# First pass of a two-layer graph kernel: the row gather adds in place onto the edge features

## The reference

```
h   = relu(layernorm(x))
msg = h[src] + edge_attr                       # first pass: node row plus edge row
agg = segment_sum(msg, dst)
x   = x + batchnorm(relu(agg @ W1 + b1) @ W2 + b2)
h   = relu(layernorm(x))
x   = x + layernorm_graph(gcn2(relu(gcn1(h)))) # second and third pass: weighted sums of h[src], no edge features
```

## Time and profile before

| what | us |
|---|---|
| median of 3 runs (lowest to highest) | 2736.61 (2732.78 to 2737.00) |
| the profiled execution | 2731.35 |
| its span from first to last instruction | 2730.00 |
| PE busy | 2450.0 |
| POOL busy | 1920.0 |
| DVE busy | 1509.8 |
| ACT busy | 1323.0 |

### The profile page before, as it was taken

One profiled execution on the slowest core, in us unless ns is written; L12 is line 12 of the kernel. 1 busy time (PEld: TensorE's weight loads), 2 busy tenths in 40 slices (PEclk: granted clock), 3 DMA queues, 4 the chain that ended last, 5 costly groups with the idle time before them and its releaser, 6 DMA issues.

```text
span 2730.0 us, 67333 instructions
## 1 busy us (share of the span) xinstructions
PE 2450.0 (90%) x26318; PEld 2369.3 (87%) x26318; DVE 1509.8 (55%) x3805; ACT 1323.0 (48%) x3271; POOL 1920.0 (70%) x1833
## 2 busy tenths in 40 slices
PE   1399899999999999965999999999969999999996
PEld 0298899888898889855999999999969999999996
DVE  8898899888898889844333433333302222222212
ACT  8588788888888888855432433423200000000001
POOL 5777877777777777702777777777437777777772
PEclk9999999999999999967999999999979999999998
DMA  4566566666566666636566565665676666565654
GB/s 111 134 179 175 168 178 175 169 187 177 162 184 179 184 170 175 176 113 206 196 230 201 186 221 191 198 219 180 216 194 211 209 216 214 198 205 190 211 197 140
DMA packets 339567, 506.63 MB, mean 186 GB/s; under 512 B 277602, under 2 KB 283160, under 8 KB 313905
## 3 DMA queue, kind: packets, MB, share of 16 engines
q1 hardware_dynamic: 270454, 292.79, 34.4%
q0 software_dynamic: 57952, 89.89, 14.7%
q10 hardware_dynamic: 10840, 119.53, 11.6%
HBM read 364.94 MB, written 137.13 MB: 184 GB/s over the span
## 4 chain that ended last, share of the span: by engine, by line
PE 55%; POOL 19%; DVE 8%; issue 7%; ACT 6%; DMA 4%; SPq 1%; DVEq 0%; ACTq 0%; POOLq 0%
PE psum L1118 38%; POOL arena L1297 19%; PE psum L1098 5%; PE psum L1140 4%; PE psum L1133 3%; DMA arena<-in_edge_attr_dram 3%; ACT arena L1230 2%; DVE arena L964 2%; ACT arena L1217 1%; PE psum L1076 1%; DVE arena L990 1%; PE psum L1153 1%; DMA arena<-table,srcT 1%; PE psum L1156 1%; SPq L1312 1%
## 5 line engine op out<-in xcount | busy, mean ns | idle before, releaser
L1297 POOL DMA_INDIRECT arena<-table,srcT x1770 | 1839.9, 1040 | 650.2 <-issue 606.6
L1118 PE MATMUL psum<-arena 125*125 125x193 bf16 (+1 forms) x19600 | 1974.5, 247 | 44.4 <-DMA arena<-counts 22.9
L1118 PEld LDWEIGHTS psum<-arena 125*125 125x125 fp8e4 x19600 | 1860.1, 137 | 53.3 <-DMA arena<-counts 23.3
L1230 ACT ACTIVATE arena<-psum 125x500 uint16<-125x500 f32 (+1 forms) x923 | 662.9, 718 | 436.1 <-PE psum L1098 431.8
L1217 ACT ACTIVATE arena<-iota,modT 128x125 uint8<-128x125 f16 x1775 | 602.9, 391 | 2.1 <-ACT arena L1230 2.1
L964 DVE TENSOR_SCALAR arena<-iota,keyT,oddT 128x300 f16<-128x300 f16 x1775 | 575.7, 357 | 22.3 <-PE psum L1098 18.8
L1098 PE MATMUL psum<-arena 128*125 128x300 f16 x1775 | 524.2, 297 | 54.5 <-ACT arena L1230 34.1
L1279 ACT ACTIVATE cneg<-cst 125x1 f32<-125x1 f32 x25 | 5.1, 203 | 689.3 <-DVE arena L1051 689.3
L1098 PEld LDWEIGHTS psum<-arena 128*125 128x125 fp8e4 x1775 | 243.4, 137 | 100.2 <-DVE arena L964 70.8
L974 DVE SCALAR_TENSOR_TENSOR arena<-relT,psum 128x960 bf16<-128x960 f16 x272 | 308.9, 1136 | 0.0
L990 DVE TENSOR_TENSOR arena<-arena 128x650 f32<-128x650 f32 x334 | 273.0, 817 | 14.2 <-DMA arena<-in_edge_attr_dram 13.9
(11 more groups left out here) (222 smaller groups left out, 1014.1 us busy)
## 6 DMA issues: line engine op xcount, KB each, us to landing
arena<-counts SPq DMA_DIRECT2D x125, 1600.0 KB
counts<-arena ACTq DMA_DIRECT2D x71, 1600.0 KB
arena<-in_edge_attr_dram SPq DMA_DIRECT2D x166, 320.0 KB
arena<-table,srcT POOLq DMA_INDIRECT x1770
table<-arena SPq DMA_DIRECT2D x8, 1050.0 KB
table<-arena SPq DMA_DIRECT2D x25, 168.0 KB
arena<-table SPq DMA_DIRECT2D x4, 1050.0 KB
arena<-in_x_dram ACTq DMA_DIRECT2D x4, 700.0 KB
```

The lines of the kernel that those rows point to most:

```text
L1118: last = pe.matmul(ps_v[n % 2][0:PN, 0:xc], A(slot)[0:PN, j, 0:PN], Xs[0:PN, j, 0:xc], start=(j == 0), stop=(j == J - 1))
L1230: act.activation(A2(slot)[0:PN, :, i // 2 * NWORD:i // 2 * NWORD + n_w], ps_b[at % NBANK][0:PN, 0:n_w * J].rearrange("p (x j) -> p j x", j=J),
L1297: pool.indirect_dma_start(out=gbuf(slot)[0:parts, t, :], out_offset=None, in_=tables[k], in_offset=bass.IndirectOffsetOnAxis(ap=idx, axis= ...
```

## The change: the gather adds onto the edge features

In pass 0, the table in DRAM holds the fp32 rows themselves (64 x 4 B = 256 B) instead of three bf16 parts. It is stored from `H` as soon as the rows are normalised. For a gathered group SP loads the edge features first, into one of three blocks of its own (`NSUM`). POOL waits for that load (`d_pre`) and issues 10 indirect DMAs with `compute_op=ALU.add`, which add the node rows onto the edge rows in SBUF. DVE splits the sums into parts (rest1 now waits for `d_sum`, all adds landed, and for the products of the gathered group before, since all gathered groups share the two blocks of the second and third part). PE multiplies S with these parts once; L1140's products are gone from pass 0. Groups without a gather keep the two old buffers. The edge loads of the first three gathered groups stand ahead of all others in SP's list; later ones are due 2.5 steps behind the product of the gathered group three before. POOL starts its table arithmetic only when the table is stored. Passes 1 and 2 stay as they are.

```diff
+NSUM = 3
+SUM_A, SUM_FROM, SUM_STEP, SUM_R = (0, 3, 6), (0, 2, 2), (2, 1, 2), (2, 4)
...
         if k == 0:
-            sp.append((t - 12.5, "edges", n))
+            with_sum = [m for m in range(n) if groups[m] in with_gather]
+            if g not in with_gather:
+                sp.append((t - 12.5, "edges", n))
+            elif len(with_sum) < NSUM:
+                sp.append((-50.0 + n, "edges", n))
+            else:
+                sp.append((first + with_sum[-NSUM] * (total - first - 3) / len(groups) + 2.5, "edges", n))
...
-        tables = [nc.dram_tensor(f"table{k}", [N, 3 * F], BF16, kind="Internal").ap() for k in range(3)]
+        tables = [nc.dram_tensor("table0", [N, F], F32, kind="Internal").ap()]
+        tables += [nc.dram_tensor(f"table{k}", [N, 3 * F], BF16, kind="Internal").ap() for k in range(1, 3)]
...
+        def sp_first_table():
+            for i, c in enumerate(LN_ORDER):
+                j0, j1 = chunk[c]
+                if c >= 2:
+                    sp.wait_ge(m_tnrm, i + 1)
+                else:
+                    sp.wait_ge(m_nrm, c + 1)
+                for p0, p1 in bands():
+                    sp.dma_start(tables[0].rearrange("(p j) f -> p (j f)", p=PN)[p0:p1, j0 * F:j1 * F],
+                                 H[p0:p1, j0 * F:j1 * F]).then_inc(st_tab, 16)
...
             if k == 0:
                 for q in range(NEDGE):
                     V(dve.memset(ebuf(q).rearrange("p (t f) -> p t f", f=FE)[:, :, F:FE], 1.0))
+                for q in range(NSUM):
+                    V(dve.memset(sblock(SUM_A[q]).rearrange("p (t f) -> p t f", f=FE)[:, :, F:FE], 1.0))
...
                 elif kind in ("rest1", "rest2"):
...
+                    if v in plain:
+                        e = plain[v] % NEDGE
+                        whole, rest = ebuf(e, i), ebuf(e, i + 1)
                     else:
+                        e = sum_of[v]
+                        whole = sblock(SUM_R[0] if i else SUM_A[e % NSUM])
+                        rest = sblock(SUM_R[i])
+                    if i == 1:
                         dve.wait_ge(v_rest1, v + 1)
+                    elif v in plain:
+                        dve.wait_ge(d_edg[e], (plain[v] // NEDGE + 1) * 16)
+                    else:
+                        dve.wait_ge(d_sum[e % NSUM], sum_done[e])
+                        if e >= 1:
+                            dve.wait_ge(p_q, pl["gats"][e - 1] + 1)
...
-                    gathered = v in pl["gat_of"]
+                    gathered = k > 0
...
+                        parts3 = e3(plain[v] % NEDGE) if v in plain else sum3(sum_of[v] % NSUM)
                         for t in range(nt):
-                            last = pe.matmul(ps_q, S[0:parts, t, :], e3(v % NEDGE)[0:parts, t, :, :],
-                                             start=(t == 0), stop=(t == nt - 1 and not gathered))
+                            last = pe.matmul(ps_q, S[0:parts, t, :], parts3[0:parts, t, :, :],
+                                             start=(t == 0), stop=(t == nt - 1))
...
+        def pool_add(i):
...
+            pool.wait_ge(d_pre[i % NSUM], (i // NSUM + 1) * 16)
+            to = sblock(SUM_A[i % NSUM]).rearrange("p (t f) -> p t f", f=FE)
+            for t in range(nt):
+                idx = srcT[:, t, g - G0:g - G0 + 1] if g < G else src_l[0:R, t:t + 1]
+                pool.indirect_dma_start(
+                    out=to[0:parts, t, 0:F], out_offset=None, in_=tables[0],
+                    in_offset=bass.IndirectOffsetOnAxis(ap=idx, axis=0),
+                    compute_op=ALU.add).then_inc(d_sum[i % NSUM], 16)
...
+                    else:
+                        i = sum_of[v]
+                        if i >= NSUM:
+                            sp.wait_ge(p_q, pl["gats"][i - NSUM] + 1)
+                        to, landed = sblock(SUM_A[i % NSUM]), d_pre[i % NSUM]
...
             pool.wait_ge(v_rest, NCH)
+            pool.wait_ge(st_tab, NCH * NBAND * 16)
```

More of the change, by code:

```diff
@@ L405, in bass_gnn_preln_kernel @@
         d_edg = [sem(f"d_edg{i}") for i in range(NEDGE)]
+        d_pre = [sem(f"d_pre{i}") for i in range(NSUM)]
+        d_sum = [sem(f"d_sum{i}") for i in range(NSUM)]
         d_cnt = [sem(f"d_cnt{i}") for i in range(NA)]
@@ L908, in bass_gnn_preln_kernel @@
         last_b = {}
+        plain = {n: i for i, n in enumerate(n for n in range(NG) if n not in plans[0]["gat_of"])}
+        plain_at = list(plain)
+        sum_of, sum_done = plans[0]["gat_of"], []
+        for i, n in enumerate(plans[0]["gats"]):
+            sum_done.append((sum_done[i - NSUM] if i >= NSUM else 0) + 16 * shape(order0[n])[1])
         for k in range(3):
             pl = plans[k]
-            for i, n in enumerate(pl["gats"]):
+            for i, n in enumerate(pl["gats"] if k else ()):
                 slot = (pl["g0"] + i) % NSLOT
@@ L1858, in sp_first @@
             sp_load()
-            sp_table(0, LN_ORDER)
+            sp_first_table()
             sp.wait_ge(a_turn, N_TURN)
```

75 lines of the change are left out of this document (47 added, 28 removed).

## The result

| | before | after |
|---|---|---|
| median of the runs, us | 2734.70 (2732.72 to 2737.00, 4 runs) | 3120.49 (3116.30 to 3122.59, 4 runs) |
| ratio | 1 | 1.1405, interval 1.1386 to 1.1425 |
| profiled execution's span, us | 2730.0 | 3120.5 |
| POOL's stream of pass 0, first issue to last end, us | 106.19 to 1155.60 | 112.33 to 1541.16 |
| from one DMA of it to the next | 1.474 | 2.008 |

I had said 2810 (2720 to 3150). The time lies in the range, but the step from 2735 is +386 us, where I forecast +75. The direction came out, and so did the reading that POOL's stream sets the pass; the price of an add, five times what I had taken, did not.

A forecast was written before the change was run, and what follows sets the result against it. The prediction took POOL's gather stream to bound pass 0. Adds at +78 us and the stream's end at -3, start included, gave +75 on 2736.6, so 2811, stated as 2810 us, range 2720 to 3150.

The forecast's parts named there:

- What bounds pass 0: Pass 0: POOL, never free, issues 711 gathers, one every 1.474 us; its stream alone is 1048 us.
- rival B: Pass 0: faster, since PE's 59 us come out; 2678 us, or part of the way up to 2731; chance 0.14.
- Start of the stream, +6: POOL's first add in pass 0 must wait for edge rows; starts at 112 instead of 106.19, +6 us (+3 to +10).
- DVE and ACT at nothing, later passes as they were: DVE and ACT keep their instruction numbers and stay under POOL's 1048 us, 0 us; passes 1 and 2 as long as now.
- rival D: Pass 0: POOL waits 2 us for edge rows in half of the 69 later groups, +69 us, 2803; chance 0.10.
- Transfers are not the bound: DMA engines: with the gathers' queue share of 15.7% doubled, the total share goes from 0.63 to about 0.79, below 1.
- End of pass 0, -3 with the start in it: Behind POOL's last adds: PE's last product comes at 1173.1 instead of 1176.12, -3 us (-7 to +2), later start included.
- Price of an add, 0.11 us: POOL's DMAs in pass 0: only the part exposed to DVE grows by half, 0.11 us each, 712 times, +78 us.
- my signs of being wrong: Wrong if pass 0 gets shorter by more than 10 us, or if POOL is seen to wait for products or edges.
- My bound of 0.58 us: Bound on an add's extra price on POOL, if all of a gather's time is list and grows by half; +413 us.

The follow-up runs named there:

- e2: The kernel before with nine of the ten products on gathered rows left out in each gathered group of pass 0; 2737.78 us, ratio 1.0010.
- e1: The changed kernel with the ten indirect DMAs of a gathered group copying the node rows instead of adding them; 2752.82 us, ratio 1.0071.
- e3: The changed kernel with SP's reload of x held back until the last products of pass 0 are done; 3105.33 us.
- e5: The changed kernel with 66 instead of 58 windows of pass 0 built without the gather, leaving 582 adds; 2859.26 us, ratio 1.0461.
- e9b: The changed kernel with rest1 and rest2 of pass 0 done over 65 of 650 numbers; 3047.07 us, ratio 1.1133.
- bench_add: Separate program of POOL's indirect DMAs alone, copy or add, over row counts, widths and beside DVE work; 128 rows: copy 0.945 us, add 1.541.
- e6: The kernel before with nine of ten products on gathered rows left out and rest1 and rest2 over 65 of 650 numbers; 2660.44 us, ratio 0.9729.

## Where the prediction was right, and the step that failed

**What bounds pass 0: right.** I had read POOL's 79% with nothing but 0.3 us gaps as full. e2 shows it by itself: 53 us off PE, 2737.78 us. That also settles rival B, whose 59 us were PE's.

**Start of the stream, +6: right.** The first add came at 112.33, forecast 112.

**DVE and ACT at nothing, later passes as they were: right.** 947 and 924 us; pass 1's gathers 961 ns on the mean, as in the earlier trace rows.

**Edge rows in the middle of the pass (rival D): refuted.** After the first add, POOL had no wait but its 0.3 us.

**Transfers are not the bound: right, by a wide margin.** The adds' queue from 300 to 1500 us:

```profile
q0 software_dynamic: 85930, 19.59, 18.9%
```

Against the earlier trace rows, 0.189 x 16 x 1200 us over 597 adds of 128 rows is 47 ns a row; before, 0.157 x 16 x 700 us over 476 gathers was 29. An added row takes 1.6 times as long on the DMA engines as a copied one of one and a half times the bytes, and the share of all engines still fell, 0.63 to 0.54. The packets differ too: 85,930 for 76,416 added rows, more than one for each, where the earlier trace rows has 15,219 for 60,928 copied rows, one for four. It is the adding and not the width of 256 B, as e1, which copies such rows, shows from 300 to 1000 us:

```profile
q0 software_dynamic: 14912, 15.30, 10.6%
```

That is 20 ns a row over 467 copies, again with one packet for four rows.

**End of pass 0, -3 with the start in it: wrong, by a term I did not list.** The last product came 26 us behind the stream's end (1567.3 against 1541.2), where my figures give 11.8; e3, with the reload held back, has 12.1, and e5, where it went out later by itself, 11.5. So the sum from the last add to the last product was right, with some luck: in e3 the last full group's product came 3.5 us behind its last add where I had 6, and the last product 12.0 behind that one where I had 8.5. The reload of x, which in the kernel after went out between, cost 15 us more. In e9b it did so again: issued at 1466.5, with rows of the last full group there 15.0 us behind its last add (1466.75 to 1481.76).

**Price of an add, 0.11 us: this is the step that failed.** The prediction put it so: "Since rows of any size take the same 0.94, I leave that part alone and let only the part exposed to DVE grow by half". The measured difference is 0.534 us a DMA, and it is made the other way round. The 0.94 grew to 1.54 (bench_add: 0.945 to 1.541, nothing beside it), and the part that DVE causes shrank, from 1.169 - 0.94 = 0.23 to 1.703 - 1.54 = 0.16 (e6 against e2, and e9b against after, have 0.19 and 0.10 of it for the rests alone). 711 x 0.60 = +427 and 711 x (-0.07) = -50 make up the 711 x 0.534 = +380, but for rounding. Behind it was a wrong inference: that the price did not depend on the size of a row showed only that the bytes are not in it. It said nothing of the number of entries, nor of the kind of operation, and these two are what the add changes. None of my signs of being wrong would have caught this: the pass did not get shorter, and POOL waited for neither products nor edges.

My bound of 0.58 us, if all of a gather's time were list and grew by half, came within 0.05, but by luck: the price is 0.46 fixed and about 1 ns a row, with the DVE part going down. Only the second piece is like a list that grows: 0.9 ns a row to 2.0.

**The two rules.** The Trainium skill, SBUF — State Buffer, section "SBUF: two separate sides", names two kinds of VectorE operations that take the port shared with GpSimd: those in a mode with two ports, and those with two SBUF inputs, the latter only against a GpSimd operation that reads SBUF. I had cited the first kind for L990, which has two SBUF inputs. The runs agree in that such a subtraction holds up GpSimd's indirect DMAs (a copy +0.34 us). I used the rule to argue that a longer list is stopped more often; the runs show less delay for an add on the mean, 0.12 us. The Trainium skill, Collectives: The Full Stack, section "The bandwidth ceiling: the fold count and why AG ≠ RS ≠ AR", has two read descriptors for a reduction where a copy has one. The price per row, 0.9 to 2.0 ns, goes that way, but the fixed 0.46 us is in neither rule, and for the engine that issues it, adding was not free.

**What the saving was worth.** Of the two sides of the change the profile shows this balance: PE lost 712 products, some 59 us, worth nothing that the time shows; each of the 712 DMAs got 0.534 us dearer, all of it on the path.

**Left open.** Why a copy gets dearer when PE is ahead (1.169 to 1.188 in e2, to 1.202 in e1) with DVE's work unchanged: I have no run that tells whether it is the order in which DVE's work meets POOL's. What the fixed 0.46 us consists of; whether the larger number of packets has a part in it, no run shows. And why an add is caught by a subtraction less often than a copy, but for longer.

## What to carry to other kernels

An engine whose every gap is the same 0.3 us put down to "issue" is full, whatever its busy share says; taking work from its neighbours brings nothing, and what makes each of its instructions dearer is paid in full. When a change puts a form of instruction that no trace shows on that engine 700 times, its price decides everything: measure it by itself before anything else, over rows, width and beside the work that will run next to it, since the price of a relative that looks alike (0.94 us) says little. Look for what slows that engine from outside: here half of DVE's SBUF subtractions was worth 0.8%, and nine tenths of the work in them, with room on PE, 2.7%, both at the price of inexact or incomplete sums.

## What the runs showed of the hardware that I had not expected

- An indirect DMA that adds costs GpSimd 1.54 us for 128 rows, one that copies 0.945; for 16 rows 1.31 and 0.84; 64, 256 or 512 bytes a row make no difference. Without a list 24 DMAs of 128 x 256 B took 14.6 us, with adding 21.1.
- GpSimd's DMAs are slowed by VectorE's subtraction of two SBUF operands (0.945 to 1.29, add 1.54 to 1.66), not by fp16 work from SBUF to SBUF at 91% busy (0.973), nor by work with a PSUM input (0.951). In the kernel the copy's mean follows them: 1.083 with one a group and 1.169 with two; with fewer products on PE 0.996 with short ones, 1.188 and 1.202 with two, 1.267 with 72 additions besides.
- On the DMA engines a 256 B row took 47 ns when it was added, in a packet of its own, and 20 ns when it was copied, four to a packet.
- Two loads (2.8 and 0.3 MB) issued on SP at 1537.11 put the landing of adds issued up to 1537.84 off from 1.6 us to 16.5; held back until the last product, they gave 15.2 us back.
